# Float32r half-array pairs in two cross-attentions, and another head for the stage between them

## What is computed

```python
# second block (q = normed x, k = v = ctx_1024), 16 heads of width 16
qh = _split_heads(q @ wq.T + bq, B); kh = _split_heads(k @ wk.T + bk, B); vh = _split_heads(v @ wv.T + bv, B)
scores = jnp.einsum('bhqd,bhkd->bhqk', qh, kh) / math.sqrt(D_K)
scores = jnp.where(mask == 0, jnp.float32(-1000000000.0), scores)
attn = jax.nn.softmax(scores, axis=-1)
out = jnp.einsum('bhqk,bhkd->bhqd', attn, vh).transpose(0, 2, 1, 3).reshape(B, -1, D_MODEL) @ wo.T + bo

# fourth block: 8 query heads of width 128, one key and one value
Q = jnp.einsum('bnd,hdk->bhnk', x, proj_q); K = jnp.einsum('bmd,dk->bmk', x, proj_k); V = jnp.einsum('bmd,dv->bmv', x, proj_v)
O = jnp.einsum('bhnm,bmv->bhnv', jax.nn.softmax(jnp.einsum('bhnk,bmk->bhnm', Q, K), axis=-1), V)
Y = jnp.einsum('bhnv,hdv->bnd', O, proj_o)

# fifth block: keys and values from the context row of the largest score
qp = jnp.einsum('bld,ed->ble', q, Wq)
idx = jnp.argmax(jnp.einsum('bld,bmd->blm', qp, kv), axis=-1)
mem = jnp.take_along_axis(kv, idx[..., None], axis=1)
mk, mv = jnp.split(jnp.einsum('bld,ed->ble', mem, Wkv), 2, axis=-1)    # one key and value head of width 16
logits = jnp.einsum('bhld,bmd->bhlm', qh, mk) * scale                  # 16 query heads
out = jnp.einsum('bhlm,bmd->bhld', jax.nn.softmax(logits, axis=-1), mv)
```

## Time and profile before

| | us |
|---|---|
| median of three runs | 996.01 |
| the profiled execution | 992.95 |
| its span, first to last instruction | 991.2 |
| first cross-attention, first score to last value product | 151.0 to 376.8 |
| shared stage, first instruction to the next stage's first score of the context | 497.6 to 699.7 |
| second cross-attention, first score to last value product | 726.1 to 854.9 |

### The profile page before, as it was taken

One profiled execution on the slowest core, in us unless ns is written; L12 is line 12 of the kernel. 1 busy time (PEld: TensorE's weight loads), 2 busy tenths in 40 slices (PEclk: granted clock), 3 DMA queues, 4 the chain that ended last, 5 costly groups with the idle time before them and its releaser, 6 DMA issues. The chain is left out here.

```text
span 991.2 us, 13446 instructions
## 1 busy us (share of the span) xinstructions
PE 891.3 (90%) x4350; PEld 492.0 (50%) x4354; DVE 669.6 (68%) x1367; ACT 503.0 (51%) x997; POOL 326.5 (33%) x329
## 2 busy tenths in 40 slices
PE   5888888999999987799969999998988999869996
PEld 2445554333323334366756888787432232534575
DVE  5865668888899933455456777775689987445654
ACT  3886454677777772012125665553216878342321
POOL 7326536200000001156416666563330000125823
PEclk9999999999999998699879999999998999959999
DMA  5040027022222902833320000000200550075200
GB/s 156 1 159 0 1 50 113 8 51 50 50 50 64 325 1 71 321 138 120 111 68 1 1 1 1 1 1 1 79 3 12 198 198 1 1 262 195 69 18 27
DMA packets 41657, 73.83 MB, mean 74 GB/s; under 512 B 8964, under 2 KB 27780, under 8 KB 40436
## 3 DMA queue, kind: packets, MB, share of 16 engines
q1 hardware_dynamic: 36372, 59.68, 19.6%
q0 software_dynamic: 4400, 13.11, 4.3%
q10 hardware_dynamic: 816, 0.17, 0.1%
HBM read 49.67 MB, written 10.49 MB: 61 GB/s over the span
## 5 line engine op out<-in xcount | busy, mean ns | idle before, releaser
L1081 DVE TENSOR_REDUCE c_amx<-PS 128x1 f32<-128x512 f32 x256 | 158.9, 683 | 26.6 <-PE PS L981 26.4
L1174 ACT ACTIVATE c_aE<-PS 128x512 f32<-128x512 f32 x256 | 132.6, 603 | 47.1 <-PE PS L993 46.9
L1861 POOL TENSOR_SCALAR s_Pn<-s_Pr,s_rs 128x512 f32<-128x512 f32 x64 | 100.1, 1568 | 75.4 <-DVE s_rs L1903 75.2
L72 POOL TENSOR_SCALAR rstd<-mv 128x4 f32<-128x4 f32 x8 | 1.9, 232 | 336.6 <-DVE mv L95 336.5
L981 PE MATMUL PS<-c_aKs,c_aQs 99*128 99x512 bf16 x256 | 96.0, 384 | 5.2 <-DMA c_aQs<-area 3.6
L993 PE MATMUL PS<-c_aQs,c_aKs 99*128 99x512 bf16 x256 | 94.5, 380 | 3.5 <-ACT c_aE L1174 2.3
L1081 DVE TENSOR_REDUCE h_amx<-PS 128x1 f32<-128x512 f32 x128 | 79.5, 683 | 8.6 <-PE PS L981 8.3
L1174 ACT ACTIVATE h_aE<-PS 128x512 f32<-128x512 f32 x128 | 67.5, 601 | 21.6 <-PE PS L993 21.3
L1992 ACT ACTIVATE s_Pr<-PS,s_nmx 128x512 f32<-128x512 f32 x64 | 44.1, 690 | 63.0 <-DVE s_nmx L1896 62.9
L1004 PE MATMUL PS<-c_aE,c_VB 128*17 128x512 f32 x512 | 67.4, 598 | 0.1
L981 PEld LDWEIGHTS PS<-c_aKs,c_aQs 99*128 99x128 bf16 x256 | 24.8, 97 | 79.0 <-DVE c_amx L1081 55.7
(11 more groups left out here) (495 smaller groups left out, 1982.7 us busy)
## 6 DMA issues: line engine op xcount, KB each, us to landing
area<-in_e_w SPq DMA_DIRECT2D x16, 512.0 KB, 9.7
area<-in_g_w SPq DMA_DIRECT2D x8, 1024.0 KB, 6.4
c_aKs<-area SPq DMA_DIRECT2D x48, 128.0 KB
g_B<-in_g_b SPq DMA_DIRECT2D x1, 4096.0 KB, 14.1
c_aQs<-area SPq DMA_DIRECT2D x48, 64.0 KB
h_aQs<-h_QP SPq DMA_DIRECT2D x48, 64.0 KB
early<-in_ctxT SPq DMA_DIRECT2D x2, 1024.0 KB, 7.3
e_B<-in_e_b SPq DMA_DIRECT2D x1, 2048.0 KB
```

The lines of the kernel that those rows point to most:

```text
L1081: dve.tensor_reduce(self.mx[:, qt, j, half:half + 1], PS[:, n % MB, :], AX.X, ALU.max).then_inc(self.max_done, 1)
L1174: act.activation(self.E[kt % 2][:, j, :], PS[:, MB + x % XB, :], ACT.Exp, scale=0.25).then_inc(self.exp_done, 1)
L1861: pool.tensor_scalar(Pn[g % NPB][:, :], Pr[g % NPB][:, :], rs[:, g % NPB:g % NPB + 1], None, ALU.mult).then_inc(pn_ready, 1)
```

## The change

In `Attention`: queries and keys become float32r. Each is split in two parts, and three products of parts are laid under each other, 3 x 16 rows, with the 3 tail rows ahead of them: 51 rows. Even heads of a unit stand in partitions 0 to 50, odd ones in 64 to 114. The score of head j is followed by the transposed score of head j ^ 1, so that neighbours stand on different halves of the array. Scores use a ring of four banks, in which the output transposes take a place too; transposed scores use a ring of three, in which the maxima transposes, the late values (first cross-attention) and the second batch's keys (second) take places; values use bank 6. Scores run a unit and two steps ahead. The maxima transposes move one step forward. Their result is copied once, whole, by ACT to `MTs`, and SP spreads it to the four heads' tail rows by four transfers (`tails`), for which PE waits before a unit's first transposed score. The output copy moves from step 0 to the middle of step 1, the normalisation between the second and the third reduction of step 2. The second conversions (`second_part`, `far_second`, `R`) go. SP's constant tail comes from SBUF, after a transfer and a wait of its own (`load_tail`). In the second cross-attention the expert weights are loaded from ACT's queue, in units 1 to 4.

In `shared_kv_stage`: keys, values and the first query are plain float32 products of the transposed x; the values are made inside the loop's first four steps; the splitting of `wq` is moved to DVE (high) and POOL (low, by head), that of x to DVE and POOL, the low part of `wo` in eight pieces into the loop's first eight steps.

```diff
-NBLK = 6
-TAIL = NBLK * HD
+NBLK = 3
 TAIL_ROWS = 3
-ROWS = TAIL + TAIL_ROWS
+HALF = P // 2
+ROWS = TAIL_ROWS + NBLK * HD
+PAIRS_H = GH // 2
...
-MB, XB = 3, 3
+MB, XB, VALUE_BANK = 4, 3, 6
...
+        self.out_steps = [(u, min(GH * ((u + 2) * self.C + 4), GH * UNITS * self.C)) for u in range(UNITS)]
+        specials = [(0, "m", 0)] + [((u * self.KT - 1) * GH, "m", u) for u in range(1, UNITS)]
+        specials += [((u * self.KT + kt + 1) * GH, "extra", i) for i, (u, kt) in enumerate(extras)]
...
+    def wait_max_bank(self, pe, item):
+        before = item - MB
+        if before < 0:
+            return
+        for u in range(UNITS):
+            if self.out_item(u) == before:
+                pe.wait_ge(self.o_normed, u + 1)
+                return
+        pe.wait_ge(self.max_done, before + 1 - sum(self.out_item(u) < before for u in range(UNITS)))
...
-        n = (u + 1) * self.C + kt + 1
+        n = (u + 1) * self.C + kt + 2
...
+    def tails(self, sp, u):
+        sp.wait_ge(self.t_copied, u + 1)
+        for j in range(GH):
+            sp.dma_start(self.Qs[u % self.NQ][tail_of_head(j), j // 2, :].bitcast(F32),
+                         self.MTs[32 * j:32 * j + TAIL_ROWS, :].bitcast(F32)).then_inc(self.tails_in, 16)
...
+            r = rows_of_head(j)
+            pe.matmul(self.max_bank(item), self.Qs[u % self.NQ][r, j // 2, qt * P:(qt + 1) * P],
+                      self.Ks[self.key_buffer(u)][r, j // 2 % self.KP, half * BANK:(half + 1) * BANK],
                       start=True, stop=True).then_inc(self.s_done, 1)
...
+            j = x ^ 1
+            r = rows_of_head(j)
+            if kt == 0 and x == 0:
+                pe.wait_ge(self.tails_in, 16 * GH * (u + 1))
...
-                if kt == KT - 1 and u + 1 < UNITS:
-                    if before_maxima:
-                        before_maxima(pe, u)
+                if kt == KT - 2 and u + 1 < UNITS:
                     maxima_transposes(u + 1)
...
-                    maxima(v, c)
+                    maxima(v, c, range(GH // 2))
+                if kt == 2 and u > 0:
+                    normalise(u - 1)
+                if v is not None:
+                    maxima(v, c, range(GH // 2, GH))
                     if c == C - 1:
                         negated(v)
-                if kt == KT - 1 and u + 1 < UNITS:
-                    upper_tails(u + 1)
-                if kt == 2 and u > 0:
-                    normalise(u - 1)
...
+            act.activation(self.MTs[:, :], self.exp_bank(self.special_item("m", u)).bitcast(BF16)[:, 0:S],
+                           ACT.Copy).then_inc(self.t_copied, 1)
...
-KEY_SLOTS = ((0, 3, 5), (1, 4), (2,))
-QUERY_SLOTS = ((0, 1, 2), (3, 4), (5,))
+KEY_SLOTS = ((0, 1), (2,))
+QUERY_SLOTS = ((0, 2), (1,))
...
+                if 1 <= u <= ExpertWeights.EXP // 2 and kt % 2 == 0:
+                    sh.weights[1].load_expert(act, 2 * (u - 1) + kt // 2)
...
-            pe.wait_ge(w_ready, 2)
             for b in range(B):
-                pe.wait_ge(xkv_ready, KD * (b + 1))
+                pe.wait_ge(xf_ready, KD * (b + 1))
                 for k in range(KD):
-                    last = products(PS[:, 4 + b, :], [w[:, k, :] for w in wks], [x[:, k, b * S:(b + 1) * S] for x in XTs],
-                                    k == 0, k == KD - 1)
+                    last = pe.matmul(PS[:, 5 + b, :], wk[:, k, :], XT[:, k, b * S:(b + 1) * S],
+                                     start=(k == 0), stop=(k == KD - 1))
                 last.then_inc(kv_mm, 1)
+            for k in range(KD):
+                last = pe.matmul(PS[:, 4, :], wq[:, 0, k, :], XT[:, k, 0:S], start=(k == 0), stop=(k == KD - 1))
+            last.then_inc(q_mm, 1)
...
                 if g < G:
                     scores(g)
+                if g < VP:
+                    values(g)
```

More of the change, by code:

```diff
@@ new lines, in wait_exp_bank @@
+    def wait_exp_bank(self, pe, item):
+        before = item - XB
+        if before < 0:
+            return
+        for at, what, i in self.specials:
+            if self.special_item(what, i) == before:
+                if what == "m":
+                    pe.wait_ge(self.t_copied, i + 1)
+                else:
+                    self.extra_free(pe, i)
+                return
+        pe.wait_ge(self.exp_done, before + 1 - sum(self.special_item(w, i) < before for _, w, i in self.specials))
@@ L1053, in step @@
                     meanwhile(pe, kt, KT)
-        for c in range(C + 1):
+        for c in range(C + 2):
             for j in range(GH):
@@ L1140, in vector @@
         negated(0)
-        maxima(1, 0)
-        if between:
-            between()
-        upper_tails(0)
+        for c in range(2):
+            maxima(1, c)
         for u in range(UNITS):
@@ L1151, in scalar, with copy_maxima @@
         PS, KT = self.PS, self.KT
-        def tails(u):
+        def copy_maxima(u):
             act.wait_ge(self.mT_done, u + 1)
-            for j in range(GH // 2):
-                act.activation(self.Qs[u % self.NQ][TAIL:ROWS, j, :],
-                               PS[32 * j:32 * j + TAIL_ROWS, 7, :].bitcast(BF16)[:, 0:S],
-                               ACT.Copy).then_inc(self.q_ready, 1)
+            if u > 0:
+                act.wait_ge(self.tails_in, 16 * GH * u)
+            act.activation(self.MTs[:, :], self.exp_bank(self.special_item("m", u)).bitcast(BF16)[:, 0:S],
+                           ACT.Copy).then_inc(self.t_copied, 1)
         def copy_output(u):
@@ L1325 @@
     NK = 1024
[L1326 removed]
+    RING = (6, 5, 3, 4)
     FIRST = 2
@@ L1397, in cross_stage @@
     VB = sb("VB", [P, UNITS, KT, GH, VW])
-    loads = 1 + sum(map(len, KEY_SLOTS)) + 1 + sum(map(len, QUERY_SLOTS))
-    at = Attention(nc, ctx, stage, PS, "c_a", NK, GH, sh.ident, sh.identb, loads)
+    loads = 2 * (1 + sum(map(len, KEY_SLOTS)) + 1 + sum(map(len, QUERY_SLOTS)))
+    at = Attention(nc, ctx, stage, PS, "c_a", NK, GH, sh.ident, sh.identb, loads, (0, 1, 2, 7), (3, 4, 5),
+                   extras=[(u, 3) for u in range(UNITS // B)])
     at.V = VB
@@ L1446, in part, with rounded @@
         return QP[p][:, m, b * S:(b + 1) * S]
+    def rounded(what, n, p):
+        return part(what, n, p).bitcast(F32R)
     def value_rows(t):
@@ L1593, in first_part @@
             def first_part(c, f):
-                act.activation(part(*c, 0), f, ACT.Copy).then_inc(p0_ready, 1)
+                act.activation(rounded(*c, 0), f, ACT.Copy).then_inc(p0_ready, 1)
             def far_first(i):
@@ L1602, in far_first @@
                 first_part(far[i], F[i % 4])
-            def far_second(i):
-                act.wait_ge(far_r_ready, i + 1)
-                act.activation(part(*far[i], 1), R[i % 4], ACT.Copy).then_inc(p1_ready, 1)
             def take_queries(n):
@@ L1656, in _ @@
             far_first(8)
[L1657 to L1661 removed]
+            for t in range(4, KT):
                 take_values(t)
@@ L1953, in _ @@
         def _(act):
-            act.activation(wqs[0][:, :, :, :], wq[:, :, :, :], ACT.Copy).then_inc(wqh_ready, 1)
             for g in range(KD * B):
@@ L2081, in project @@
                     last.then_inc(y_mm, 1)
-            for k in range(KD):
-                query_part(0, k)
             for g in range(STEPS):
@@ L2269, in _ @@
                     sp.wait_ge(at.av_done, (u - NQ + 1) * at.KT)
-                    tails(u)
-                for p in range(3):
+                    at.first_tails(sp, u)
+                for p in range(2):
                     if n == 0:
-                        sp.wait_ge((p0_ready, p1_ready, p2_ready)[p], 1)
+                        sp.wait_ge((p0_ready, p1_ready)[p], 1)
                     else:
-                        sp.wait_ge(far_p2_ready, n)
+                        sp.wait_ge(far_p1_ready, n)
                     query_part(u, p)
-                if u >= NQ:
-                    for e in range(2 * (u - NQ), 2 * (u - NQ + 1)):
-                        sh.weights[1].load_expert(sp, e)
+            for u in range(NQ):
+                load(u)
+            for u in range(UNITS):
+                at.tails(sp, u)
+                if u >= 1 and u + NQ - 1 < UNITS:
+                    load(u + NQ - 1)
         @block.gpsimd
@@ L2392, in _ @@
                 first_part(n)
-            for n in range(KD):
-                second_part(n)
             for k in range(KD):
@@ L3347, in layouts @@
     A["m_wout"] = ktile(I["L0_attn_out_proj_w"].T)
-    one = 0x3F80
-    A["q_tail"] = np.repeat(np.array([[0], [0], [one]], np.uint16), GH * S, 1)
+    A["q_tail"] = np.repeat(np.array([[0], [0], [1]], np.float32), PAIRS_H * S, 1)
     A["ctxT"] = I["ctx_1024"].transpose(2, 0, 1).reshape(KD, P, -1).transpose(1, 0, 2)
```

470 lines of the change are left out of this document (238 added, 232 removed).

## The result

| | before | after | predicted |
|---|---|---|---|
| median of four runs, us | 996.49 (995.84 to 997.32) | 1055.76 (1048.74 to 1058.84) | 987 (967 to 1002) |
| ratio to before, 95% interval | | 1.058 (1.053 to 1.064) | 0.991 |
| profiled execution (its span) | 992.95 (991.2) | 1055.6 (1053.8) | |
| mean granted clock of the span | 0.956 | 0.907 | |

The account below looks back on a forecast made before the run. PE was taken to bound the kernel, with DVE close behind. First cross -1, second cross +4 and the shared stage's head -12 sum to -9 us, from a median of 996.01 to 987, range 967 to 1002.

Parts of the forecast that it names:

- rival B: Attentions: array halves do not overlap, eight starts make 1.9 us, step 2.96; 1006 us, slower; chance 0.12.
- PE's step of 2.05: First cross, plain step: 0.96 matmuls, 0.1 gap and 0.99 values on PE, below DVE's 2.48 us.
- The walk of one unit: First cross: DVE's 21.2 us plus 2.55 idle behind bank, transfer and output waits make 23.7; 23.5 taken, before 23.83.
- Term (c): Unit change: PE waits for SP's four tail transfers, 0.36 us an issue and 2.2 landing; 0.5 idle on DVE.
- Rival C: Unit changes: tails' transfers land 1 us later in each of 14, so 987 becomes 1001 us; chance 0.13.
- A unit with late values adds the same 1.8 in both kernels: First cross: units in which late values are made cost 1.8 us more, before and after the change alike.
- rival D: Attention steps: PE needed 2.05 of 2.9 us, so clock may fall; step 3.9, some +60 us; chance 0.03.
- Start: First cross's first score: constant tail's load and wait, then eight small transfers, move it from 151.0 to about 152.7 us.
- one more step without scores: End of the first cross: one added step remains after the scores, 2.4 us.
- Second cross: Units 13.5 us against 13.11, weight loads on ACT +0.3 and +0.4 a unit, run-up gives back 1: +4 (-6 to +10).
- The head of the shared stage: First score 15.4 us earlier, less 2.8 for values and 0.6: net -12 us, from -9 to -14.
- Rival A: Attentions: DVE binds alone, transfers under 2 us, rings hide waits; units 22.2 and 12.1; 966 us; chance 0.17.

Follow-up runs that it names:

- filled stands: Changed kernel plus matmuls by zeros ahead of three PE waits in each unit (six, four and five; four ahead of the tails' transfers); 1032.2 us, ratio 1.035.
- no transfers: Changed kernel without the tails' transfers and PE's wait for them, with zero matmuls ahead of the two bank waits (six and five); 1008.8 us, ratio 1.012.
- the new head alone: Kernel before with only the changed kernel's `shared_kv_stage`; 984.56 us, ratio 0.987.
- the normalisation first: Changed kernel with GpSimd copies for the tail transfers, and DVE normalising before step 2's four reductions; 999.3 us, ratio 1.004.
- more work elsewhere: Changed kernel plus 14 matmuls by zeros a unit at the start of step 3, where PE does not stand; 1091.9 us, ratio 1.098.
- the last experiment: GpSimd tail copies, earlier normalisation and filled late-values wait on the changed kernel, plus 24 spare matmuls ahead of the first cross's first score; 994.3 us, ratio 0.999.
- the overlap undone: Changed kernel with each score followed by the transposed score of the same head, not its neighbour's; 1090.6 us, ratio 1.094.
- the kernel before with gaps: Kernel before with four more DVE reductions before the fourth chunk's first one in units 1 to 7, 14 gaps; 1033.8 us, ratio 1.037.

## Why the prediction was wrong, point by point

*The sum against the runs.* The forecast had the attentions at +3 (-1 and +4); they are +71. Three steps lead from the changed kernel to the one with only the new head, each the difference of two medians:

| | us |
|---|---|
| changed kernel, 1055.8, to filled stands, 1032.2: clock | 23.6 |
| to no transfers, 1008.8: the tails' path | 23.4 |
| to the new head alone, 984.6: rings, late values, start and end | 24.2 |

*Overlap of the halves: right, and rival B (no overlap) wrong.* Pairs start together.

*PE's step of 2.05: wrong.* It is 2.62. The fourth transposed score waits for the first one's exponential (ring of three), and the values start 0.43 behind it, not 0.1. DVE, at 0.63 to 0.64 a reduction, needs 2.5 to 2.6, so this hid in DVE's time, and with the normalisation first the units come near DVE's own time. But the reserve of 0.4 a step which the walk gave PE does not exist.

*The walk of one unit: right but for one term.* At the high clock (the run with less filling) the unit is 25.56, predicted 23.5. The stand for output copy and transposes is 1.48 (walked 1.45), the one around the normalisation 0.72 (0.6). DVE's own time is 25.56 less 3.88 of stands, 21.7 (21.2). Term (c), the transfers, is 1.51, not 0.5.

*Why (c) failed.* The issue of a tail transfer was priced at 0.36, after four small transfers in 1.43. Four tail transfers take 2.84, 0.71 each (0.64 and a gap). SP's row in the changed kernel:

```profile
279.10 2.84 SPq L1052 DMA_DIRECT2D c_aQs<-c_aMTs  x4
```

ACT's copy ends at 279.07, PE is released at 283.15: 4.1 us, where the walk had 3 x 0.36 + 2.2 = 3.3. The last issue starts at 281.30, 1.1 us later than priced, and PE is released 1.85 behind it, a little sooner than the 2.2 taken (from rows that were no small transfers inside SBUF either). The issue is what was wrong. Its row was the nearest by size and not by kind: those four come from an input in device memory, while the query transfer between two buffers in SBUF beside them cost 0.59. Rival C had this effect, priced at 1 us in each of 14 unit changes, and only for another reason.

*The late values: a missing wait.* "A unit with late values adds the same 1.8 in both kernels" is wrong. Their bank now stands in the exponential ring, and PE waits 1.3 for ACT's copy. A unit with them costs 3.2 more than one without at the high clock (27.3 against 24.1), 1.8 before. Four such units: 5.6 us.

*The clock: the step that failed most in kind.* All durations were warm ones, with rival D at 0.03 for "steps may fall to the low level" because PE would be needed for 2.05 of 2.9 us. In the first attention it was not mainly the plain steps' share of work that dropped it (more work elsewhere left 58 of 72 us low), but stands of 0.9 to 3 us, most of which the walk itself had listed as waits of PE. Filling them took the low level from 126 to 30 us and the time down by 23.6, 0.25 us for each. D's price of some +60 was too high by more than half, and that the kernel did come out 59 us above the one before is coincidence: the clock is well under half of it. My reading after the result (48 us, 0.34 for each) was too high too. A second price needs no filling. The executions of one kernel differ in their granted clock: over the 70 of the thirteen kernels other than the one before, with each kernel's own mean taken off, an execution is 0.30 us longer for each us more at the low level (an estimate from span and mean clock; 95% interval 0.26 to 0.34). By it the 96 us are worth 25 to 33, of which the filling takes some back. Why it is less than the half that a step bound by PE alone would lose was only argued: in part of the low time PE would have stood anyway.

*Start.* SP's extra wait and issues made PE stand 6.11 instead of 3.62 ahead of the first score: +2.5, predicted +1.7. What wasn't predicted is that this longer stand drops the clock for the run-up, 4.3 us more; the last experiment took that away.

*End.* From the last unit's output the walk counted "one more step without scores", 2.4. Steps without scores take 2.59 (values at 424.72 and 427.31 in the changed kernel's PE timeline; 372.20 and 374.58 before, 2.38), for the same ring of three. What the 24.2 left over hold is seen in the distances of the run filled and without transfers against the run with the head alone. First cross: the stage's start to its first score +3.0, the run-up +5.6 (low clock), the first unit +3.9, the three other units with late values +1.65 each, those without +1.4 in all, the end +4.4 (the added step of 2.6 and 1.8 of slower ones). Second cross: run-up and first unit -2.7, the unit in which PE waits for the second batch's keys +3.3, five more units +0.8, the end +3.5. That is 28; the first cross's stage began 5.2 us sooner in that trace, which is the scatter named above. Some 24 us more at the low level than in the run with the head alone are in it too.

*Second cross.* Predicted +4, measured +22. At the high clock the unit is 14.69 to 14.98 with the transfers and 13.32 without (predicted 13.5 to 14.2), the same in units with and without weight loads on ACT: the 0.7 a unit that I put on these was not there.

*The head of the shared stage: right.* -12.4 for -12, and alone -11.9 of 996.5 (-12.9 against the 997.43 beside it).

*Rival A* (966) was the nearest to what the idea can do: without transfers and with the normalisation first the units come to 22.86 and 12.22, predicted for it 22.2 and 12.1. But even then other places take back more than that brings. In the last run, from first score to last output transposes, the first attention takes 238.2 us for 226.5: the first unit costs 5.8 more (most of it the stand for GpSimd's copies), the end 7.1, the three units with late values 1.3 in all, and the three without give back 2.3. The second attention gains 2. So the best version found is still the kernel before with the new head, 984.6; copies that GpSimd makes ahead of its additions were not tried.

## What to carry to other kernels

When a change relieves the bound engine, list the stands that it will have and ask what the granted clock does behind each; a walk that finds waits of about a microsecond on TensorE has no right to warm durations alone. Before an experiment is read as "the overlap undone", look in its trace whether the overlap is gone. Price each issue of a DMA by a row of the same kind (source and destination in SBUF, same queue), not by the nearest in bytes. Before a special buffer joins a short ring, ask who frees it and how long the next user stands.

## What the runs showed of the hardware

Matmuls with 51 rows on two halves of the array start together, at either clock level (0.23 and 0.43 from pair to pair). The Trainium skill ("TensorE: Matmul & The Clock Gate", Part 3: Packing small matmuls) says this of row groups, and the trace now agrees. Which stand drops the granted clock is open: of two of 1.30 us at the same place of two units one did and one did not, and in the kernel before with gaps it fell behind three of seven in the first attention. Matmuls by zeros in the stands took the low level from 126 to 30 us; six of them in the stand of 1.53 us cost nothing that shows (a unit is 24.1 with them and without), while eight for four in the stand of 0.98 cost 0.8 a unit. Four copies of 3 x 512 on GpSimd between partitions took 2.62 and landed in time, but for the first unit, where four transfers of the same rows took 4.1. A weight load of 128 columns takes 0.10 us for the bfloat16 queries and keys (trace of before, PEld of L981), 0.18 to 0.19 for float32r (of before L2005, of after L1071), and two such loads go with each pair at 0.23.
